# Softplus of a Mamba block: the bias moves into the matrix product, the maximum to VectorE, 1 + w to ScalarE

## The reference, cut to what matters

```python
x = x + 0.5 * ffn(layernorm(x))        # 8 routed experts and a shared one
x = x + ssm(layernorm(x))              # the part the change touches
x = x + 0.5 * ffn(layernorm(x))

def ssm(x, W_x, W_dt, b_dt, A_log, D):           # x: 4 x 512 x 256
    dt_x, Bm, Cm = split(x @ W_x.T, [64, 80])    # 64 + 16 + 16 columns
    dt = softplus(dt_x @ W_dt.T + b_dt)
    dA = exp(dt[..., None] * -exp(A_log))        # 16 states
    h_t = dA_t * h_(t-1) + dt_t * Bm_t * x_t     # over 512 steps
    y_t = sum_n h_t[n] * Cm_t[n] + x_t * D
    return y
```

## Time and profile before

| | |
|---|---|
| time, median of 3 runs | 507.84 us (507.39 to 508.14) |
| the profiled execution: span from first to last instruction | 512.9 us |
| the profiled execution's own time | not given apart from its span, which is 5.1 us above the median of the runs |
| busy in the span | PE 438.5, DVE 342.4, ACT 260.3, POOL 292.6 us |
| TensorE clock granted, mean | 0.943 of full speed |
| the recurrence on DVE, L1126 | 64 x 2278 ns |
| the product on POOL, L408 | 63 x 2370 ns |
| the scan stage | 173 to 384 us |

### The profile page before, as it was taken

How to read it: one execution, slowest core, us unless ns; L and a number is a source line. 1 busy time by engine, 2 the same in 40 slices (tenths; PEclk the granted TensorE clock), 3 DMA queues, 4 the chain that set the end, 5 groups by cost and what they waited for, 6 DMA issues and landing times. The chain is left out here.

```text
span 512.9 us, 7182 instructions
## 1 busy us (share of the span) xinstructions
PE 438.5 (85%) x2264; PEld 309.2 (60%) x2264; DVE 342.4 (67%) x552; ACT 260.3 (51%) x499; POOL 292.6 (57%) x226
## 2 busy tenths in 40 slices
PE   5988899999779597659868886877999999999995
PEld 5855455555334465558767666766984656555553
DVE  5557333333386666988899989999996593333332
ACT  1210233332116669986999999997851111333331
POOL 4302366663324137698799879986891005776463
PEclk9869999999977899989979997998999999999999
DMA  8943122210312012214213331232220298333221
GB/s 286 385 154 92 35 63 65 63 59 32 125 39 64 1 61 65 83 42 105 84 61 97 87 89 63 100 100 69 85 81 1 73 328 280 97 112 103 63 61 39
DMA packets 37667, 49.90 MB, mean 97 GB/s; under 512 B 5498, under 2 KB 26814, under 8 KB 37632
## 3 DMA queue, kind: packets, MB, share of 16 engines
q1 hardware_dynamic: 32368, 38.91, 24.2%
q0 software_dynamic: 5264, 10.54, 7.0%
HBM read 37.33 MB, written 16.70 MB: 105 GB/s over the span
## 5 line engine op out<-in xcount | busy, mean ns | idle before, releaser
L408 POOL TENSOR_TENSOR gs<-hs,c_sb 128x1024 f32<-128x1024 f32 x63 | 148.3, 2370 | 53.0 <-DVE hs L1126 35.5
L1126 DVE TENSOR_TENSOR_SCAN hs<-da,bank 128x1024 f32<-128x1024 f32 x64 | 145.1, 2278 | 9.8 <-PE bank L796 9.7
L796 PE MATMUL bank<-ident,dbx_t 128*128 128x128 f32 x512 | 73.7, 290 | 35.5 <-DVE hs L1126 29.3
L697 PE MATMUL bank<-w_gu,tt 128*128 x184 | 91.1, 617 | 4.1 <-ACT tt L467 4.1
L796 PEld LDWEIGHTS bank<-ident,dbx_t 128*128 128x128 f32 x512 | 60.6, 149 | 50.3 <-DVE hs L1126 39.1
L509 ACT ACTIVATE da<-dt_sb,a_neg 128x511 f32<-128x511 f32 x128 | 84.9, 713 | 7.7 <-DVE hs L1126 7.7
L363 POOL DMA_INDIRECT da<-rows,row_token x46 | 47.2, 1026 | 70.7 <-DVE row_token L1021 57.2
L523 ACT ACTIVATE dbx_t<-dtx_t,h_sb 128x256 f32<-128x256 f32 x194 | 83.8, 497 | 2.7 <-PE bank L796 2.7
L1034 DVE SCALAR_TENSOR_TENSOR q_sb<-th,bank 128x256 f32<-128x256 f32 x46 | 19.4, 421 | 90.2 <-ACT th L462 90.2
L812 PE MATMUL bank<-ident,gs 128*128 128x128 f32 x504 | 71.6, 290 | 8.7 <-POOL gs L408 8.6
L462 ACT ACTIVATE th<-bank,da 128x256 f32<-128x256 f32 x46 | 21.8, 473 | 99.2 <-PE bank L697 99.2
(11 more groups left out here) (125 smaller groups left out, 529.9 us busy)
## 6 DMA issues: line engine op xcount, KB each, us to landing
c_sb<-c_dram SPq DMA_DIRECT2D x64, 256.0 KB, 3.1
rows<-xn_no SPq DMA_DIRECT2D x12, 516.0 KB, 6.5
x_sb<-in_x SPq DMA_DIRECT2D x4, 512.0 KB, 5.8
w_gu<-in_gate_w SPq DMA_DIRECT2D x2, 1024.0 KB, 10.1
w_gu<-in_up_w SPq DMA_DIRECT2D x2, 1024.0 KB, 11.1
w_dn<-in_down_w SPq DMA_DIRECT2D x2, 1024.0 KB, 10.7
xn_no<-token_out SPq DMA_DIRECT2D x4, 512.0 KB, 5.5
rest<-x_sb SPq DMA_DIRECT2D x4, 512.0 KB, 4.9
```

The lines of the kernel that those rows point to most:

```text
L408: nc.gpsimd.tensor_tensor(gs[:, s % 2], hs[:, s % RING], c_sb[:, s % RING].unsqueeze(1).to_broadcast([P, KC, L]), ALU.mult).then_inc(sc_g, 1)
L697: last = nc.tensor.matmul(H[j % 2][:, :], tt[:, j % 2, 2 + k], w_gu[:, k, bass.ds(e, 1), :].squeeze(1), start=(k == 0), stop=(k == KC - 1))
L796: mm = nc.tensor.transpose(DBX[s % 2][:, k, i * P:(i + 1) * P], dbx_t[:, s % TURNS, i, k * P:(k + 1) * P], ident[:])
L1126: nc.vector.tensor_tensor_scan(hs[:, s % RING].rearrange(flat), da[:, s % RING].rearrange(flat), DBX[s % 2][:, :, :].rearrange(flat), 0.0, ...
```

## The change

- **The bias is a 65th row.** `proj` has 128 rows now: 64 of dt, a row of ones at 64 (written by ACT's copy, which adds column 64 of the identity as a bias; W_x is padded with zeros by a memset on POOL), B at 96 and C at 112. `w_dt` has b_dt as its 65th row. The product z already holds the bias. SP issues two DMAs for W_x instead of one, and b_dt goes to one row.
- **The maximum** is no longer written by ACT. DVE takes it from PSUM, in one instruction with the correction.
- **1 + w** is written by ACT into `dt_sb` (for batch 0 by DVE); exp is done per half.
- **DVE per half** (`project_w`): ((1 + w) - 1) - w in `dt_sb`, both inputs in SBUF; then max(z, 0) minus that.
- **The last sum** (`project_dt`) is one instruction over both halves, 1024 columns, both inputs in SBUF (for batch 0 one per half).
- **Places**: the second half's z product moves from n = 1 to n = 4, its ACT part from n = 2 to 5, ln from n = 4 to 6, `project_w` from n = 5, 7 to n = 3, 6, `project_dt` to n = 8, `turn_dt` from n = 8, 10 to 9, 11. `project_dtx` stays at 10 and 12.

```diff
-            sp.dma_start(w_x[:], w_xT.rearrange("(k p) r -> p k r", p=P)).then_inc(small_in, 16)
-            sp.dma_start(w_dt[:], w_dtT).then_inc(small_in, 16)
-            sp.dma_start(b_sb[:], b_dt).then_inc(small_in, 16)
+            w_x_rows = w_xT.rearrange("(k p) r -> p k r", p=P)
+            sp.dma_start(w_x[:, :, 0:R], w_x_rows[:, :, 0:R]).then_inc(small_in, 16)
+            sp.dma_start(w_x[:, :, B_ROW:], w_x_rows[:, :, R:]).then_inc(small_in, 16)
+            sp.dma_start(w_dt[0:R, :], w_dtT).then_inc(small_in, 16)
+            sp.dma_start(w_dt[R:R + 1, :].rearrange("o (k p) -> o k p", k=KC),
+                         b_dt.rearrange("p (o k) -> o k p", o=1), allow_slow_non_contiguous=True).then_inc(small_in, 16)
...
+            nc.gpsimd.memset(w_x[:, :, R:B_ROW], 0.0).then_inc(w_pad, 1)
...
-                nc.scalar.activation(proj, pj_bank(b, 0)[0:R + 2 * N, :], ACT.Copy).then_inc(pj_copy, 1)
+                nc.scalar.activation(proj, pj_bank(b, 0), ACT.Identity, bias=ident[:, R:R + 1]).then_inc(pj_copy, 1)
...
-                    act.wait_ge(pj_rest, KC * b)
-                nc.scalar.activation(w_exp[:, k], pj_bank(b, k), ACT.Abs, bias=b_sb[:, k:k + 1]).then_inc(pj_abs, 1)
-                nc.scalar.activation(dt_sb[:, k, seq(b)], pj_bank(b, k), ACT.Relu, bias=b_sb[:, k:k + 1]).then_inc(pj_max, 1)
-
-            def project_exp(b):
-                act.wait_ge(pj_abs, KC * (b + 1))
-                nc.scalar.activation(w_exp[:], w_exp[:], ACT.Exp, scale=-1.0).then_inc(pj_exp, 1)
+                    act.wait_ge(pj_rest, KC * (b - 1) + k + 1)
+                nc.scalar.activation(w_exp[:, k], pj_bank(b, k), ACT.Abs).then_inc(pj_abs, 1)
+                act.wait_ge(pj_abs, KC * b + k + 1)
+                nc.scalar.activation(w_exp[:, k], w_exp[:, k], ACT.Exp, scale=-1.0).then_inc(pj_exp, 1)
+
+            def project_u(b, k):
+                act.wait_ge(pj_exp, KC * b + k + 1)
+                nc.scalar.activation(dt_sb[:, k, seq(b)], w_exp[:, k], ACT.Copy, bias=1.0).then_inc(pj_u, 1)
...
+                for k in (range(KC) if b == 0 else (slice(0, KC),)):
+                    nc.scalar.activation(log_w[:, k], w_exp[:, k], ACT.Ln, bias=1.0).then_inc(pj_ln, 1)
...
-                    late = int(b == 0)
-                    if more and n in (1 + late, 2 + late):
-                        project_abs(b + 1, n - 1 - late)
-                    if more and n == 3 + late:
-                        project_exp(b + 1)
-                    if more and n == 4 + late:
+                    for k in range(KC):
+                        if more and n == ((1, 5), (2, 5))[b == 0][k]:
+                            project_abs(b + 1, k)
+                            project_u(b + 1, k)
+                    if more and n == 6:
                         project_ln(b + 1)
...
-                nc.tensor.matmul(pj_bank(b, k), w_dt[:, k * P:(k + 1) * P], proj[0:R], start=True, stop=True).then_inc(pj_z, 1)
+                nc.tensor.matmul(pj_bank(b, k), w_dt[:, k * P:(k + 1) * P], proj[0:R + 1], start=True, stop=True).then_inc(pj_z, 1)
...
-                    late = int(b == 0)
-                    if more and n in (late, late + 1):
-                        project_z(b + 1, n - late)
+                    for k in range(KC):
+                        if more and n == ((0, 4), (1, 4))[b == 0][k]:
+                            project_z(b + 1, k)
...
-                    if more and n in (8, 10):
-                        turn_dt(b + 1, (n - 8) // 2)
+                    if more and n in (9, 11):
+                        turn_dt(b + 1, (n - 9) // 2)
...
             def project_w(b, k):
 
-                if k == 0:
-                    dve.wait_ge(pj_exp, b + 1)
-                    dve.wait_ge(pj_max, KC * (b + 1))
-                elif b > 0:
-                    dve.wait_ge(pj_dt, KC * b + 1)
-                nc.vector.tensor_scalar(pj_bank(b, k), w_exp[:, k], 1.0, -1.0, ALU.add, ALU.add).then_inc(pj_w, 1)
-                dve.wait_ge(pj_w, KC * b + k + 1)
-                nc.vector.tensor_tensor(pj_bank(b, k), w_exp[:, k], pj_bank(b, k), ALU.subtract).then_inc(pj_rest, 1)
+                dt = dt_sb[:, k, seq(b)]
+                if b == 0:
+                    dve.wait_ge(pj_exp, k + 1)
+                    nc.vector.tensor_scalar(dt, w_exp[:, k], 1.0, None, ALU.add).then_inc(pj_u, 1)
+                dve.wait_ge(pj_u, KC * b + k + 1)
+                nc.vector.scalar_tensor_tensor(out=dt, in0=dt, scalar=-1.0, in1=w_exp[:, k],
+                                               op0=ALU.add, op1=ALU.subtract).then_inc(pj_rest, 1)
+                dve.wait_ge(pj_rest, KC * b + k + 1)
+                nc.vector.scalar_tensor_tensor(out=dt, in0=pj_bank(b, k), scalar=0.0, in1=dt,
+                                               op0=ALU.max, op1=ALU.subtract).then_inc(pj_max, 1)
 
             def project_dt(b, k):
 
-                dve.wait_ge(pj_ln, b + 1)
-                dve.wait_ge(pj_rest, KC * b + k + 1)
-                nc.vector.tensor_tensor(pj_bank(b, k), log_w[:, k], pj_bank(b, k), ALU.add).then_inc(pj_sum, 1)
-                dve.wait_ge(pj_sum, KC * b + k + 1)
-                nc.vector.tensor_tensor(dt_sb[:, k, seq(b)], pj_bank(b, k), dt_sb[:, k, seq(b)], ALU.add).then_inc(pj_dt, 1)
+                dve.wait_ge(pj_max, KC * b + (k + 1 if b == 0 else KC))
+                dve.wait_ge(pj_ln, k + 1 if b == 0 else KC + b)
+                nc.vector.tensor_tensor(dt_sb[:, k, seq(b)], log_w[:, k], dt_sb[:, k, seq(b)],
+                                        ALU.add).then_inc(pj_dt, 1 if b == 0 else KC)
...
-                    if more and n in (5, 7):
-                        project_w(b + 1, (n - 5) // 2)
-                    if more and n in (6, 8):
-                        project_dt(b + 1, (n - 6) // 2)
+                    if more and n in (3, 6):
+                        project_w(b + 1, (n - 3) // 3)
+                    if more and n == 8:
+                        project_dt(b + 1, slice(0, KC))
```

35 lines of the change are left out of this document (18 added, 17 removed).

## The result

| | before | after |
|---|---|---|
| median of 6 runs each, same chip | 507.99 us (506.08 to 519.68) | 520.62 us (517.0 to 522.97) |
| ratio, 95% interval | | 1.025 [1.0213, 1.0287] |
| profiled execution: span, own time | 512.9, own time not listed | 519.2, 520.96 |
| mean granted clock of it | 0.943 | 0.937 |

The change is slower. Forecast were 514.2 us in a range of 506.4 to 519.3; the median came out above the range, and the loss is twice the forecast one (12.6 us for 6.4). An execution's own time is 1.7 to 1.8 us above its span, wherever both are listed.

What follows compares the result with a forecast made beforehand. DVE was taken to bound the scan (52.17 of 54 us busy), with POOL and PE one wait away. Batches 0 to 2 add 1.6 + 2.4 + 2.4 = +6.4 us to 507.84: 514.2 us, range 506.4 to 519.3.

Steps and rivals of the forecast that it cites:

- the last one of the sum: Final step: the runs' median lies 5.1 us below the profiled span, so +6.4 us is added to 507.84, giving 514.2.
- the walk: Step-by-step count of the scan's batches in the old trace's times: 1.6 + 2.4 + 2.4 = +6.4 us.
- n = 3 costs 0: Batch 1: the correction goes ahead of POOL's product, the next recurrence starts as before; DVE idle 0.1 before B's copy.
- The corrections at n = 6: Batches 1 and 2: the correction waits 2.3 us for POOL's product, so n = 7 starts 1.0 later.
- The sums: Last sum at n = 8 of batches 1 and 2: waits 1.9 us for POOL's queued product.
- waits for the port: DVE instructions with two SBUF inputs wait for POOL's instruction: 11.5 us of waits in all, making 7.9 us of time.
- n = 9 and the turns: Batch 1: n = 9 starts 1.5 us later; DVE then waits 0.45 twice for PE's turn, +0.9. Batch 2 as much.
- Batch 0: First batch: DVE waits 4.8 us for the second turn behind a late add, a stall of 2.29 goes; +1.6 us.
- first rival: The new DVE instructions do not wait for POOL: -1.45 us, 506.4 us, faster; chance 0.22.
- second rival: POOL keeps the port while it has instructions queued: corrections at n = 6 wait longer, 8 us more, 522 us; chance 0.08.
- ACT as the bound: ACT, with 3.0 us free in 54, becomes the bound; dependent steps could cost 0.3 more; within the range, no own chance.
- What would show it: Profile signs: correction 0.69 to over 2 us, sum 1.2 to 3.5, turn waits 0.4 and over 4, B's copy waits 0.1.

Runs made afterwards that it cites:

- turn_ahead: Changed kernel with PE's turn of dt put ahead of the add that waits for POOL: scan 195.71 us, median 512.5 us against 508.25 for the kernel before.
- after_again: Changed kernel, no edit, profiled and timed a second time: scan 201.36 us, median 527.88 us against 519.72 for the kernel before on the same chip.
- before_turn_late: Kernel before with only turn_dt moved to n = 9 and 11: scan 197.19 us, +4.0 against before; 526.95 us (1 run) against 520.76.
- one_sbuf: Changed kernel, correction and last sum reading one SBUF and one PSUM operand (wrong results): scan 199.75 us, median 519.28 us against 508.25 for before.
- ahead_corr: Changed kernel, turn ahead of the add and only the correction reading PSUM plus one SBUF operand (wrong results): scan 194.07 us, 527.27 us (1 run) against before's 519.72.
- ahead_skip: Changed kernel, turn ahead of the add and PE's skip products at n = 6: scan 195.95 us, 528.52 us (1 run) against 520.73 for before.

## Why the prediction was wrong

**The step that failed** is the last one of the sum: "The median lies 5.1 below that span; I carry the difference over unchanged." The profiled execution of before had a late start (173.47) and the median one an early start (167); nothing ties the two. The 5.1 below the span (6.8 below the execution's own time, if that is 1.76 above its span as in all of after's runs) showed that before had more than one usual time, and I did not ask which of them the change would meet. A term of a few microseconds for the start should have been in the range, and not the 0.2% that the prediction took as what a measurement can tell: executions of before lie between 501.5 and 520.1 us on one chip. This step is 4.1 of the 6.2 us that were missing. The other 2.1 are the walk: from the first recurrence to the last it is 8.5 us longer in after's first profile (7.3 from n = 3), for 6.4. Of its two terms that of the port was mis-sized most: priced at 7.9 us, it measured 0.8 to 1.6, as told below. That the spans lie 6.3 apart looks like a hit and is chance: 8.5 less the 2.2 by which that execution of after began its scan earlier.

Point by point, as differences of the recurrences' starts between the first two profiles:

1. **n = 3 costs 0**: right for the correction (0.67, first at the port). "The next recurrence starts as before" and 0.1 ahead of the copy: wrong, 1.58 and 1.74. PE stood idle 2.5 us for the recurrence and then worked at half its pace. In the trace of turn_ahead it waited as long and did not. The two, after and turn_ahead:

```profile
252.70 1.97 PE L802 MATMUL bank<-ident,dbx_t 128*128 128x128 f32 x8 [2.51 <-DVE hs L1134]
254.46 1.69 PE L818 MATMUL bank<-ident,gs 128*128 128x128 f32 x8
```
```profile
244.65 1.09 PE L802 MATMUL bank<-ident,dbx_t 128*128 128x128 f32 x8 [2.52 <-DVE hs L1134]
245.58 1.04 PE L818 MATMUL bank<-ident,gs 128*128 128x128 f32 x8
```

The granted clock from n = 3 to n = 5 was 0.80 and 0.81 in the two batches of after, and 1.00 in batch 1 of turn_ahead. The walk had no term for this. It added 1.5 and 1.6 us to n = 5 of the batches 1 and 2. Little of it is lost in the end: in turn_ahead n = 4 to 5 of batch 1 is 1.48 shorter than in after, and n = 6 to 7, where the correction waits for POOL, 1.45 longer.

2. **The corrections at n = 6**, 2.3 each: 0.6 and 2.8. As n = 6 came 1.5 later than in the walk, it met POOL's products at another phase. 3. **The sums**, 1.9 each: 1.7 and 0.2. In batch 0 I had 2.0 for the correction at n = 6; it waited 0.5 for POOL, and 1.20 for ACT's 1 + w before that, for which the walk had nothing. All waits for the port within the scan come to 6.7 us (the six corrections 4.5 over 0.66 to 0.68, the three sums 2.2 over 1.20), where I had 11.5.

4. and 5. **n = 9 and the turns**: batch 1 forecast +1.5 and +0.9; +0.9 and +1.6 were measured. Batch 2 +2.4 in sum, +2.6 measured. These sums are right by luck, as errors cancel in them: more for the copy of B, less for the port.

6. **Batch 0**, +1.6: +2.8 up to n = 2 of batch 1. The wait of 4.8 for the second turn was 5.76, and the first turn, for which the walk had none in this batch, was waited for too (1.27, behind PE work at the lower clock). The correction at n = 3 behaved as forecast, 1 + w arriving late, with 0.1 left of it at n = 5 (forecast 0.3).

**The division was wrong, though the sum was near.** I priced the waits for the port at 7.9 us of time. Taken away by themselves they were worth 0.8 (1.6 against after_again), and 3.7 with the turn out of the way. The turn was priced at 0.9 per batch and a wait of 4.8 in batch 0, and for a kernel in which nothing waits for the port this is right: before_turn_late shows 0.86 in the batches 1 and 2 and a wait of 4.85. In the change's arithmetic it is more, 4.8 in after. The *first rival* (no waits for POOL) had 1.45 us faster; one_sbuf is just this case and was 6.5 slower in the scan. Only with the turn moved as well did its number appear (-1.2), in a kernel that the rival did not describe. I had read 0.45 for the turn from "DVE has only a recurrence in between", in a stretch where POOL was on time. In one_sbuf DVE is at n = 9 of batch 1 1.2 us earlier than in before, ahead of POOL's products, and then waits 0.98 for `turn_dbx` and 2.27 for the first turn: when POOL is behind DVE, `add` and turn are as late as POOL.

One more slip is in the range. Between the first rival and the walk, 11.5 us of waits count as 7.9 of time; for the ends of the forecast (510.4 and 519.3) each microsecond of wait counts in full. At the first rate they would have been 511.6 and 517.7.

The *second rival* (POOL keeps the port) was right in single instances: one correction of 3.42 started at 317.06 and ended 0.5 after POOL's second product, whose start lay between, and the sum of 5.01 in ahead_corr did the same. Most others went behind the first product. What decides it no run shows. *ACT as the bound* did not come: DVE waited for ACT in batch 0 alone, 4.6 us for 1 + w in all.

**What would show it**: shortest correction 0.66, longest over 2, the wait over 4 in batch 0, all as said. The two waits of 0.4 in each of the batches 1 and 2 were 1.04 and 0.32, and 0.32 and 0.32. Two signs were wrong: the sum was nowhere 1.2 alone (1.43 at the least), and the copy of B waited 1.6 and 1.7 for 0.1. Most signs were right and yet the time was outside the range: they test the walk, not the way from a span to a median.

## What to carry to other kernels

A profile is one execution. When its time and the median of the runs are several microseconds apart, find which stage differs before adding a difference to the median; here the scan of before began anywhere between 160.3 and 178.9 us and took the same within 0.3. Measure an edit in the stage where it acts: one profile then tells a microsecond, where six timed runs hardly told two. Take a second profile of each kernel that other differences are read against: the 0.8 between the two of after is as large as one of the effects.

When an operation is moved behind one that waits for another engine, its price is that engine's worst backlog and not the operation's own time. And when two delays meet at one place, take both away as well as each by itself.

## What the runs showed of the hardware

- A DVE instruction with two SBUF inputs that waits for a POOL instruction may be passed over by the next one of POOL. Corrections that started 0.52 and 0.55 us before the end of a product once ended 0.56 after it and once waited for the following product too (3.42 at 317.06 in after, above; a product takes 2.37). The sum of 5.01 in ahead_corr started 1.6 before the end of one product and ended 1.1 after the end of the following. In both cases the DVE instruction had started before the product that passed it, so the order of issue did not decide. Where it is not passed over it looks like this, in turn_ahead:

```profile
305.60 13.08 POOL L413 TENSOR_TENSOR gs<-hs,c_sb 128x1024 f32<-128x1024 f32 x5
307.43 1.08 DVE L1086 SCALAR_TENSOR_TENSOR dt_sb<-dt_sb,w_exp 128x512 f32<-128x512 f32 x1
```

- The same wait of 2.5 us at the same place left PE at the lower clock in one kernel and at the higher in another (eight transposes in 1.97 and 1.09 us, granted 0.50 and 1.00, its levels of 1.2 and 2.4 GHz), which decides over 1.5 us at the copy of B.
- Four projection products took 3.78 us in ahead_skip and 1.99 in turn_ahead, programs that are alike up to there; from these products to the first recurrence the granted clock was 0.71 and 0.94, the time 24.0 and 18.8 us.
- Three chips agree in before's scan to 0.3 us (192.99 to 193.24) and differ by 14 us in what follows it: 130.9 at a granted clock of 1.00, 145.0 at 0.95.
